# Gathering and adding the experts' outputs inside the layer-1 time mixing, instead of in a stage before it

## The reference, cut to what matters

```python
# third sub-layer: 8 experts, each token goes through the two with the highest router logits
logits = einsum('th,eh->te', x, router_w)
topk_logits, topk_idx = top_k(logits, 2)
combine = zeros((T, 8)).at[arange(T)[:, None], topk_idx].add(softmax(topk_logits))
hmid = gelu(einsum('th,efh->etf', x, w1) + b1)
out = einsum('eth,te->th', einsum('etf,ehf->eth', hmid, w2) + b2, combine)
x = x + out                     # <- these sums are what is moved

# fourth sub-layer, on z = (x - mean) / sqrt(var + 1e-5) of each token's row
shifted = z moved by one token
k, v, r = three mixes of z and shifted, each times a 256 x 256 matrix
wkv = a scan over the batch's 256 tokens, with exponentials of k, and v
x = x + (sigmoid(r) * wkv) @ Wo.T
```

## Time and profile before

| | |
|---|---|
| three runs, us | 3635.18, 3640.21, 3641.67 (median 3640.21) |
| the profiled execution, us | 3634.66, its span 3633.0 |
| collecting stage, 1750 to 1925 us | PE 0.00 busy, DVE 98.28, POOL 125.78 |
| time mixing, 1980 to 2280 us | PE 300.00 busy, DVE 268.56, ACT 197.84, POOL 0 |
| number of batches, of tiles | 32, 64 |

### The profile page before, as it was taken

The page is one execution under the profiler, slowest core; times in us unless marked ns, Lnnn a source line. Parts: engine busy times, 40 slices in busy tenths (PEclk is TensorE's granted clock), DMA queues, the critical chain, the costliest instruction groups (busy, mean ns, idle before and its releaser), DMA issues. The chain is left out here.

```text
span 3633.0 us, 60719 instructions
## 1 busy us (share of the span) xinstructions
PE 2876.1 (79%) x21702; PEld 2244.0 (62%) x21703; DVE 2268.1 (62%) x3977; ACT 1511.0 (42%) x2470; POOL 667.5 (18%) x640
## 2 busy tenths in 40 slices
PE   4999877777655699999206999879999999177796
PEld 3666555555445588888205888756666666166686
DVE  5554557777644211111456888879999999778542
ACT  1233244434311122222004666568888888178000
POOL 0111103333346201001570000021111110000600
PEclk9999988888855799999658999889999999699898
DMA  3000051111132444444230000000000000034444
GB/s 110 0 0 0 20 205 53 53 53 53 36 123 96 151 145 141 145 142 141 86 102 27 1 1 1 1 31 13 13 13 13 13 13 7 25 162 185 173 150 162
DMA packets 109948, 259.90 MB, mean 72 GB/s; under 512 B 15040, under 2 KB 52928, under 8 KB 101056
## 3 DMA queue, kind: packets, MB, share of 16 engines
q1 hardware_dynamic: 91712, 204.85, 16.4%
q0 software_dynamic: 18048, 52.45, 4.4%
HBM read 169.17 MB, written 88.08 MB: 71 GB/s over the span
## 5 line engine op out<-in xcount | busy, mean ns | idle before, releaser
L1765 DVE TENSOR_SCALAR e_low<-bank 128x2048 f32<-128x2048 f32 x128 | 293.1, 2290 | 37.1 <-PE bank L1637 34.0
L1159 ACT ACTIVATE cx_h<-bank,c_b 128x256 f32<-128x256 f32 x288 | 120.7, 470 | 409.6 <-PE bank L1114 409.6
L1114 PE MATMUL bank<-cx_zT,cx_w 128*128 128x256 f32 x1152 | 262.5, 381 | 1.8 <-DMA cx_w<-cw_dram 0.9
L1125 PE MATMUL bank<-c_w,cx_h 128*128 x1152 | 260.4, 379 | 0.0
L1589 ACT ACTIVATE e_low<-e_low 128x2048 f32<-128x2048 f32 x128 | 245.1, 1915 | 2.1
L1586 ACT ACTIVATE e_low<-e_low 128x2048 f32<-128x2048 f32 x128 | 243.5, 1903 | 0.0
L1114 PEld LDWEIGHTS bank<-cx_zT,cx_w 128*128 128x128 f32 x1152 | 220.3, 191 | 32.3 <-DMA cx_w<-cw_dram 1.3
L2131 PE MATMUL bank<-f_wout,fd_q 128*128 128x256 f32 x1024 | 224.2, 383 | 19.6 <-DVE fd_q L2150 19.6
L1125 PEld LDWEIGHTS bank<-c_w,cx_h 128*128 128x128 f32 x1152 | 213.6, 190 | 25.9
L2131 PEld LDWEIGHTS bank<-f_wout,fd_q 128*128 128x128 f32 x1024 | 196.7, 192 | 46.9 <-DVE fd_q L2150 19.8
L1766 DVE TENSOR_SCALAR e_high<-bank 128x1536 f32<-128x1536 f32 x128 | 223.8, 1749 | 0.0
(11 more groups left out here) (362 smaller groups left out, 6781.9 us busy)
## 6 DMA issues: line engine op xcount, KB each, us to landing
cx_w<-cw_dram SPq DMA_DIRECT2D x72, 512.0 KB, 3.2
hidden<-fu_h SPq DMA_DIRECT2D x32, 1024.0 KB, 3.9
fd_h<-hidden SPq DMA_DIRECT2D x32, 1024.0 KB, 4.8
cx_rows<-expert_rows SPq DMA_DIRECT2D x72, 256.0 KB, 3.2
slot_y<-cx_y POOLq DMA_DIRECT2D x72, 256.0 KB, 2.5
X<-x_dram SPq DMA_DIRECT2D x4, 2048.0 KB, 16.0
g_cT<-ctxT_dram SPq DMA_DIRECT2D x32, 256.0 KB, 5.4
queries<-g_qT SPq DMA_DIRECT2D x32, 256.0 KB, 6.2
```

The costliest lines, as they stand in the source:

```text
L1114: last = nc.tensor.matmul(H[k][f // 2][:, (f % 2) * GROUP_ROWS:(f % 2 + 1) * GROUP_ROWS], w1[k][:, c, f * P:(f + 1) * P], zT[k][:, c, :], ...
L1125: last = nc.tensor.matmul(Y[k][:, n * D:(n + 1) * D], h[k][:, f, n * P:(n + 1) * P], w2[:, bass.ds(e, 1), f, :].rearrange("p o d -> p (o d ...
L1159: nc.scalar.activation(h[k][:, f, :], H[k][f // 2][:, (f % 2) * GROUP_ROWS:(f % 2 + 1) * GROUP_ROWS], ACT.Gelu, bias=b1[:, bass.ds(e, 1), ...
L1765: nc.vector.tensor_scalar(flat(low[n % RING][:]), HEADS4.rearrange("p r s -> p (r s)"), -1.0, 0.0, ALU.mult, ALU.max).then_inc(neg_ready, 1)
```

## The change

`collect_slots` is gone, and so is the `row_stats` ahead of the time mixing. `slot_y`, the weights and the indices are now allocated in `build`. In `layer1_rwkv` POOL issues, after its six small memsets, all 128 gathers, four for each batch, into a ring of three batches' tiles. From the fourth batch on the gathers of a batch wait until the batch three before has been added. DVE has two new functions, `collect` and `centre`; ACT has `root`, which makes 1/sqrt(variance) of two tiles as exp(-0.5 ln(var + eps)). Five batches are done ahead of the loop, the others in it, batch b+5 in trip b.

```diff
-        collect_slots(nc, t, s)
@@ layer1_rwkv
-        TWO = range(2)
+        TWO, RING, AHEAD = range(2), 3, 5
@@ gpsimd
+            for b in range(B):
+                if b >= RING:
+                    pool.wait_ge(second_in, TB * (b - RING + 1))
+                for c in range(CHOSEN):
+                    for n in range(TB):
+                        pool.indirect_dma_start(chosen_y[b % RING][c][n][:], None, t["slot_y"],
+                                                bass.IndirectOffsetOnAxis(ap=t["slot"][:, c, b * TB + n:b * TB + n + 1], axis=0)).then_inc(chosen_in[b % RING], 16)
@@ scalar
+            def root(b):
+                own = slice(b * TB, (b + 1) * TB)
+                act.wait_ge(moments_ready, TB * (b + 1))
+                nc.scalar.activation(log_var[:, own], moments[:, own, 1], ACT.Ln, bias=t["eps"][:]).then_inc(log_var_ready, 1)
+                act.wait_ge(log_var_ready, b + 1)
+                nc.scalar.activation(rstd[:, own], log_var[:, own], ACT.Exp, scale=-0.5).then_inc(rstd_ready, 1)
+
             def normalise(b):
+                act.wait_ge(shift_ready, b + 1)
...
-            for b in range(2):
-                normalise(b)
-            for b in range(2):
-                turned(b)
-                normalise(b + 2)
+            for b in range(AHEAD):
+                root(b)
+                if b < 2:
+                    normalise(b)
+                elif b < 4:
+                    turned(b - 2)
+                    normalise(b)
...
                 if known(b - 1):
                     logarithm(b - 1)
+                if known(b + AHEAD):
+                    root(b + AHEAD)
                 if known(b):
                     exponentials(b)
@@ vector
+            def collect(b):
+                tiles = range(b * TB, (b + 1) * TB)
+                dve.wait_ge(chosen_in[b % RING], 16 * CHOSEN * TB * (b // RING + 1))
+                for c, done in enumerate((first_in, second_in)):
+                    for n in range(TB):
+                        x, tile = t["X"][:, b * TB + n, :], b * TB + n
+                        if c:
+                            dve.wait_ge(first_in, b * TB + n + 1)
+                        nc.vector.scalar_tensor_tensor(x, chosen_y[b % RING][c][n][:], t["prob"][:, c, tile:tile + 1], x, ALU.mult, ALU.add).then_inc(done, 1)
+                for n in tiles:
+                    dve.wait_ge(second_in, n + 1)
+                    nc.vector.bn_stats(spread[:, n, :], t["X"][:, n, :]).then_inc(spread_ready, 1)
+                for n in tiles:
+                    dve.wait_ge(spread_ready, n + 1)
+                    nc.vector.bn_aggr(moments[:, n, :], spread[:, n, :]).then_inc(moments_ready, 1)
+
+            def centre(b):
+                own = slice(b * TB, (b + 1) * TB)
+                dve.wait_ge(rstd_ready, b + 1)
+                nc.vector.scalar_tensor_tensor(shift[:, own], moments[:, own, 0], -1.0, rstd[:, own], ALU.mult, ALU.mult).then_inc(shift_ready, 1)
...
+            for b in range(AHEAD):
+                collect(b)
+                centre(b)
             for b in range(B + 2):
                 if known(b):
                     maxima(b)
+                if known(b + AHEAD):
+                    collect(b + AHEAD)
                 if known(b - 1):
                     ratio(b - 1)
+                if known(b + AHEAD):
+                    centre(b + AHEAD)
                 if known(b - 2):
                     add(b - 2)
...
@@ build
-            row_stats(nc, t, f"ln{n}")
+            if layer is not layer1_rwkv:
+                row_stats(nc, t, f"ln{n}")
```

More of the change, by code:

```diff
@@ L849, in layer0_experts @@
              "w2": sb("w2", [P, EX, EFC, D]), "b1": sb("b1", [P, EX, EFC]), "b2": sb("b2", [P, EX, D]),
-             "rows": nc.dram_tensor("expert_rows", (EX * EXPERT_ROWS, D), FP).ap(), "y": nc.dram_tensor("slot_y", (SLOT_GROUPS * GROUP_ROWS, D), FP).ap()}
+             "rows": nc.dram_tensor("expert_rows", (EX * EXPERT_ROWS, D), FP).ap()}
         route_tokens(nc, t, d, bank, s)
         run_experts(nc, t, d, bank, s)
-        collect_slots(nc, t, s)
 def route_tokens(nc, t, d, bank, s):
@@ L1189, in _ @@
             output(SLOT_GROUPS - 1, 1, HALF - 1)
[L1192 to L1237, removed]
@@ L1251, in layer1_rwkv @@
         shift, decay = sb("shift", [P, NT]), sb("decay", [P, DC, S])
+        chosen_y = [[[sb(f"chosen{k}{c}{n}", [P, D]) for n in range(TB)] for c in range(CHOSEN)] for k in range(RING)]
+        spread, moments, log_var, rstd = sb("spread", [P, NT, 6]), sb("moments", [P, NT, 2]), sb("log_var", [P, NT]), sb("rstd", [P, NT])
         z = [sb(f"z{k}", [P, TB, D]) for k in TWO]
@@ L1262, in layer1_rwkv @@
         names = ("w_in", "setup", "wexp", "consts", "weights", "shift", "z", "zT_raw", "zT", "k_raw", "v_raw", "r_raw", "pp", "h", "arg", "ex", "abs", "er",
-                 "ev", "state", "prod", "nd", "whole", "ln", "gate_in", "gate", "y", "o_raw", "x_done")
+                 "ev", "state", "prod", "nd", "whole", "ln", "gate_in", "gate", "y", "o_raw", "x_done", "first", "second", "spread", "moments", "log_var", "rstd")
         (w_in, setup, wexp, consts, weights, shift_ready, z_ready, zT_raw, zT_ready, k_raw, v_raw, r_raw, pp_ready, h_ready, arg_ready, ex_ready, abs_ready, er_ready,
-         ev_ready, state_ready, prod_ready, nd_ready, whole_ready, ln_ready, gate_in, gate_ready, y_ready, o_raw, x_done) = (sem(n) for n in names)
+         ev_ready, state_ready, prod_ready, nd_ready, whole_ready, ln_ready, gate_in, gate_ready, y_ready, o_raw, x_done, first_in, second_in, spread_ready, moments_ready, log_var_ready, rstd_ready) = (sem(n) for n in names)
+        chosen_in = [sem(f"chosen_in{k}") for k in range(RING)]
         K, V, R, T = bank[0:2], bank[2:4], bank[4:7], bank[7]
@@ L1270, in layer1_rwkv @@
         block = ctx.enter_context(nc.Block())
[L1271 removed]
+        INIT, CONSTS, WEIGHTS = 6, 4 + DC, 6 * DC
         known = lambda b: 0 <= b < B
@@ L1296, in normalise @@
                     n = b * TB + c
-                    nc.scalar.activation(z[b % 2][:, c, :], t["X"][:, n, :], ACT.Identity, bias=shift[:, n:n + 1], scale=t["rstd"][:, n:n + 1]).then_inc(z_ready, 1)
+                    nc.scalar.activation(z[b % 2][:, c, :], t["X"][:, n, :], ACT.Identity, bias=shift[:, n:n + 1], scale=rstd[:, n:n + 1]).then_inc(z_ready, 1)
             def turned(b):
```

9 lines of the change are left out of this document (4 added, 5 removed).

## The result

| | before | after |
|---|---|---|
| runs, us | 3635.18 to 3641.67, median 3639.92 (4) | 3542.15 to 3548.28, median 3543.85 (4) |
| ratio, 95% interval | 1 | 0.974, 0.9723 to 0.9757 |
| the profiled execution, us | 3634.66 | 3542.15, its span 3540.5 |

The kernel is 96 us faster; 3541 was predicted, with 3506 to 3585 as the range.

The account below looks back on a forecast made before the run. POOL was taken to pace the collecting stage, without PE work, and PE to bound the time mixing. States of batch 31 at 2243.0 against 2342.71 save 99.7: 3634.66 - 99.7 = 3534.96, plus 5.55, say 3541; range 3506 to 3585.

Parts of the forecast that it names:

- states of batch 0: First states in the time mixing: to begin at 1793.5 us, against 1956.87 before, 163.4 us earlier.
- first trip: Batch 0's states to batch 1's: 13.0 us, a full trip of 15.06 less the weighing and addition it lacks.
- a trip, batches 1 to 26: Loop of the time mixing, DVE the bound: 11.34 + 2.5 + 1.22 = 15.06 us; batches 2 to 26 take 376.5.
- the last five trips: Batches 27 to 31, without `collect`, bound by PE running 2.5 us ahead: 5 x 12.51 - 2.5 = 60.0 us.
- `collect`: DVE's added work per trip in the loop, additions, sums and moments: 2.5 us, at least 2.4, at most 3.6.
- delay of the addition to `X`: DVE's wait for `root` in each trip starts this addition 1.22 us later, between 0.1 and 1.6.
- saved at the states of batch 31: Last states of the time mixing: at 2243.0 against 2342.71 us, 99.7 us less.
- the cheaper case: Loop rival: `centre` finds its value ready or `collect` is cheaper; about 13.9 us a trip, 29 less, 3511; chance 0.11.
- The clock in the loop: PE's idle gaps may lower its clock each trip: counted as nothing, at most 1.7 us in 26 trips, 44 us.
- the later of two paths: Start of the time mixing: DVE's path starts the loop at 1783.9 us, PE's reaches the third product at 1787.0.
- Blocking by POOL: Loop rival: DVE stands still while gathers are issued, 108 x 0.95 = 103 us, 3643, no gain; chance 0.05.
- the 5.55 us: Whole kernel: the profiled execution before lay 5.55 us below the runs' median, added to 3534.96 to give 3540.5.

Follow-up runs that it names:

- The stage kept alone: Against the kernel before: collecting stage kept without its sums, only the statistics moved into the time mixing's loop, no gathers or additions there; 3665.38 us, ratio 1.0069.
- the exponentials first: Against the changed kernel: on ACT exponentials ahead of the logarithm and `root` behind the gate, on DVE `centre` at the trip's end; 3553.58 us, again 3555.01.
- the chip of 3688.91: The changed kernel run again, unedited, on a chip where the kernel before took 3688.91 us; 3584.99 us, ratio 0.9722.
- the run with three batches' gathers: Against the changed kernel: only the first three batches' gathers are issued, later batches add the same tiles again; 3545.28 us, ratio 0.9739.
- The shorter start: Against the exponentials first: batch 0 turned ahead of the root of batch 2, batch 4 collected inside trip 0; 3547.68 us, ratio 0.9623.

## Why the prediction was right

The mechanism was the one forecast, and the steps stood as follows (us; what the after row shows is corrected by the 2.4 of the later block where it is a point in time):

| step | predicted | measured |
|---|---|---|
| states of batch 0 | 1793.5 | 1796.12 - 2.4 = 1793.7 |
| first trip | 13.0 | 14.11 |
| a trip, batches 1 to 26 | 15.06 | 14.94, in all 373.5 for 376.5 |
| the last five trips | 60.0 | 64.2 |
| `collect` | 2.5 | 2.45 |
| delay of the addition to `X` | 1.22 | 1.27 |
| saved at the states of batch 31 | 99.7 | 94.75, or 97.2 with the 2.4 |

*The collecting stage and what it gave back.* PE had no work there and POOL set the pace, so all of it could go. The first states begin 163.2 us earlier, the last ones 97.2: 66 us were given back in the loop. The stage kept alone (3665) shows the two sides apart: with the statistics in the loop and the stage still there the kernel is 24 us slower, so the stage's removal is what pays.

*The trip.* `collect` is exact to 0.05. The two `bn_aggr`, which had no row, take 0.21 us together as the distance to the next instruction (2012.84 to 2013.05); 0.22 was taken from the copy of 128x2. DVE's wait for `root` came out at 1.11 to 1.28, where 1.14 was implied. The trip is shorter than forecast by 0.12: addition and sums take 1.39 us (2017.44 to the gate at 2018.83) instead of the 1.46 of the earlier trace rows, and the wait that went was 1.20 by the timeline, where I had taken the mean of the earlier trace rows, 1.17. That the cheaper case lay near (29 us less) was shown by the exponentials first; it needed another order on ACT than the change has.

*The first trip: mis-sized by 1.1.* I took the addition of batch b-2 out of it and let DVE go straight to the states. In trip 1 it does so, and waits there:

```profile
1808.34 0.16 DVE L1465 SCALAR_TENSOR_TENSOR d_shift<-d_moments,d_rstd 128x2 f32<-128x2 f32 x1 [1.12 <-ACT d_rstd L1258]
...
1810.23 1.22 DVE L1411 TENSOR_TENSOR d_ex<-d_ex,bank 128x1024 f32<-128x1024 f32 x1 [1.13 <-ACT d_ex L1297]
```

The states are bound by the exponentials where DVE has less to do. With the exponentials first this trip took 13.07.

*The last five trips: mis-sized by 4.2.* I let PE, idle 2.5 us in a trip, give that back once DVE has no more to collect. It can't: PE turns batch b+2 only behind the addition of batch b-2, so it never gets ahead. On the chip of 3688.91 the change had 12.77 for the first of these trips, and 62.5 for the five. So 2.5 of the 4.2 us is this error. The other 1.7 is the clock (14.46 for 12.77), which in the profiled execution had fallen just there, and in that of the run with three batches' gathers too (14.46 again). A row of PE's timeline there, the window (columns as above), and DVE's timeline:

```profile
2184.25 1.91 PE L1350 MATMUL bank<-d_zT,d_nowv 128*128 128x256 f32 x4
```

```profile
2183.80:2187.00 3.20, 3.20 (x9) 2.52 (x8) 3.20 (x4) 1.77 (x4) 0.00 (x0) 0.50 0.02 5
```

```profile
2193.63 0.69 DVE L1441 TENSOR_TENSOR X<-bank,X 128x512 f32<-128x512 f32 x1 [0.58 <-PE bank L1376]
...
2196.35 0.69 DVE L1430 SCALAR_TENSOR_TENSOR d_gate<-bank,d_whole 128x512 f32<-128x512 f32 x1 [1.24 <-ACT d_whole L1302]
...
2198.24 1.22 DVE L1411 TENSOR_TENSOR d_ex<-d_ex,bank 128x1024 f32<-128x1024 f32 x1 [1.20 <-ACT d_ex L1297]
```

PE was idle for 2.15 us ahead of this trip's turning (2182.64). Four products that take 1.03 us at the full clock take 1.91 here. Now the delay reaches DVE, which waits 0.58 for PE's output, 1.24 for the logarithm and 1.20 for the exponentials.

*The clock in the loop: between nothing and 44 us, counted as nothing.* That was right as to size. Between 1820 and 2190 us PE is idle for 2.15 us ahead of 15 of 25 turnings, once for 2.49, and for 0.63 ahead of the other nine, less than the 2.5 predicted. Windows of 2.8 us that begin 1.2 us behind the turnings at 1853.91 and 1868.79:

```profile
1855.11:1857.91 2.80, 2.80 (x15) 2.45 (x14) 2.80 (x4) 1.73 (x4) 0.00 (x0) 1.00 0.00 0
1869.99:1872.79 2.80, 2.80 (x8) 2.17 (x8) 2.80 (x4) 1.74 (x4) 0.00 (x0) 0.50 0.01 3
```

The clock was at its lower level (0.50 to 0.56) in 10 of 25 such windows, always after a gap of 2.15 us or more; behind six more gaps of 2.15 it stayed full, and what decides between the two isn't shown. After each drop PE is late, the next gap is only 0.63 us, and the clock stays full behind that. A trip with the clock down ends 15.04 us after the one before it instead of 14.88. So each drop costs 0.16 us, nine of them 1.4 us in all. It takes PE's slack and little of the trip's time. That price belongs to this trip, in which PE has slack: a drop cost 1.7 us in the first trip without `collect`, and 1.5 in the one dear trip of the exponentials first. The Trainium skill, "TensorE: Matmul & The Clock Gate", section "HAM oscillation — how this bites in real kernels", describes a loop that pays the lower clock anew because of its own waits. The trace agrees in part: the clock falls again and again, but in 10 of 25 trips and at 0.16 us each, since here PE isn't the bound.

*The start.* The forecast took the later of two paths, and PE's (1787.0 for the third product; 1789.87 - 2.4 = 1787.5 measured) was the later one. The run with gathers for three batches alone confirmed it against my own expectation for that run. The shorter start names the place: the turning of batch 0 stood on ACT behind the root of batch 2, which waits for `collect`. The two edits of that run were not separated.

*Blocking by POOL.* DVE's instructions in the loop are as long as those in the earlier trace rows: additions of `collect` 479 ns in the mean, `d_nd` 1208. The run with three batches' gathers has 478 and 1207, and the same trip. The rival was rightly given little, but for gathers only.

*What lies outside.* Behind the states of batch 31 the profiled execution took 1294.2 us (3542.15 - 2247.96), before it was 1292.0, so 2.2 more. With the 2.4 ahead of the block and the 2.5 of the terms above this is the whole difference of 7.2 us between the predicted 3534.96 and 3542.15.

*What was luck.* That 3541 lies 2.9 us from the measured median owes something to errors that cancel. The trips were forecast 3.0 us too dear in all, and the first and the last five 5.3 too cheap. And the 5.55 us added for the profiled execution's place below the median were 3.9 too many (after the change it lies 1.7 below), which hides half of the 7.2.

## What to carry to other kernels

A stage that one engine paces while TensorE has nothing to do can be worth moving into a loop bound by TensorE. What it then cost here is DVE's added work and the new wait, less the idle time DVE had, and that could be summed from rows to a per cent of the trip. In the queue of a helping engine, work whose inputs are ready and that the bound engine wants next belongs ahead of work that itself waits for the bound engine: the order of a few calls on ACT, and of `centre` on DVE, was worth 30 us here, beside the 104 that the change gave on the same chip. Slack of an engine that may not run ahead (here PE, for a bank) was not paid back at the loop's end.

## What the runs showed of the hardware

- DVE and POOL arithmetic blocked each other when both read on-chip memory, and the one that was blocked waited long: one DVE product of 1.2 us took 4.76 us beside two POOL multiplications and the first of two additions. In the mean over a stretch with 30 multiplications and 30 additions on POOL, DVE instructions with two on-chip inputs grew from 1207 to 2058, from 1225 to 1517, from 693 to 965 and from 666 to 890 ns; the scans with their inputs on chip grew from 1222 to 1446 and from 1203 to 1648. Those with a PSUM input and `bn_stats` did not grow. POOL's pair of multiplications took 2.04 us in one trip and 3.08, beside DVE's scan, in the next. The Trainium skill, "SBUF — State Buffer", section "Who interferes with whom", says that a DVE instruction with two on-chip inputs contends with a POOL instruction that reads on-chip memory. The trace agrees for POOL's arithmetic, with the numbers above.
- POOL's gathers take their indices from on-chip memory too, and held up no DVE instruction (479 and 1208 ns with them, 478 and 1207 without). The reverse shows a little: one of each four in the loop takes 1.30 to 1.31 us instead of 0.95, the one that runs while DVE goes from the first to the second product of the ratio (1998.73 and 2013.77, with DVE's second product at 1999.25 and 2014.30).
- Two of the chips are slower by 48 us for the kernel before, and by 41 us for the change. The trips are the same to 0.01 us. The last store of the experts' stage comes 28.9 us later in the change (1779.49 for 1750.59), and so does the first one (1262.4 for 1233.5): the time is lost before that stage, in the routing, where DVE's 16 copies `cr_lg` span 189.7 us for 157.1 and wait 65.1 us in seven times for what the trace calls "remote". From the last store to the states of batch 0 it takes 58.4 us instead of 45.5, again with such waits, of up to 9.4 us. The profile of the change on the faster chip has none in either place. One of them:

```profile
1833.03 1.26 DVE L1401 TENSOR_TENSOR_SCAN d_pp<-d_decay,bank 128x256 f32<-128x256 f32 x2 [6.29 <-remote]
```

  That row is of the version with the exponentials first, the timeline of its start. What these waits are, and why only these chips have them, stays open.
